# Who waits for the write of a slot of maxima: VectorE at its third fold, or ScalarE at its copy

## The reference

```
theta_x = (x[dst] - x[src]) @ theta_w.T + theta_b
phi_x   = x[src] @ phi_w.T + phi_b
e       = relu(theta_x + phi_x)
out     = segment_max(e, dst, num_segments=6250)
out     = where(isfinite(out), out, 0)
y       = layernorm(x + out)          # over the features, eps 1e-5
```

## Time and profile before

| | us |
|---|---|
| median of 3 runs (lowest, highest) | 1252.27 (1236.91, 1257.81) |
| the profiled execution's own time | 1242.66 |
| its span, from the first to the last instruction | 1240.8 |
| stage 1, up to the first fold | 111 |
| the edge loop, from the first fold (110.9) to the last (1153.0) | 1042 |
| the tail | 88 |

### The profile page before, as it was taken

One profiled execution on the slowest core, in us unless ns is written; L12 is line 12 of the kernel. 1 busy time (PEld: TensorE's weight loads), 2 busy tenths in 40 slices (PEclk: granted clock), 3 DMA queues, 4 the chain that ended last, 5 costly groups with the idle time before them and its releaser, 6 DMA issues.

```text
span 1240.8 us, 5980 instructions
## 1 busy us (share of the span) xinstructions
PE 313.0 (25%) x953; PEld 194.2 (16%) x953; DVE 518.0 (42%) x1191; ACT 274.6 (22%) x568; POOL 807.9 (65%) x840
## 2 busy tenths in 40 slices
PE   6363322444342343110000000100014342430000
PEld 5142111222121232000000000000012131210000
DVE  4002332545343454543333433543325253537698
ACT  2022132233232232321111211321101010100144
POOL 6724756766666766677765676677746667667574
PEclk9667565666566655555555555555557565656555
DMA  8567545666465665676655665776547476747264
GB/s 262 164 196 225 178 156 169 229 204 210 159 204 181 215 213 194 231 241 201 199 191 166 209 192 191 256 228 206 192 139 261 145 236 225 240 136 229 100 195 157
DMA packets 111584, 245.76 MB, mean 198 GB/s; under 512 B 19141, under 2 KB 51226, under 8 KB 111546
## 3 DMA queue, kind: packets, MB, share of 16 engines
q0 software_dynamic: 39984, 109.21, 30.8%
q1 hardware_dynamic: 71130, 135.51, 29.9%
q10 hardware_dynamic: 432, 0.66, 0.2%
HBM read 129.89 MB, written 115.45 MB: 198 GB/s over the span
## 4 chain that ended last, share of the span: by engine, by line
DVE 29%; another core or an unknown queue 27%; issue 19%; POOL 10%; PE 6%; ACT 5%; DMA 4%; DVEq 1%; SPq 0%; ACTq 0%; POOLq 0%
DVE acc L582 16%; POOL rows L315 9%; DVE hist L582 6%; ACT hist L379 3%; DMA rows<-b_table,idx 2%; DVE stats L692 1%; PE acc L411 1%; DVE a_sb L681 1%; DVE hist L689 1%; DVE reached L596 1%; DVE a_sb L676 1%; PE ps_b L427 1%; PE ps_a L411 1%; DVEq L580 1%
## 5 line engine op out<-in xcount | busy, mean ns | idle before, releaser
L315 POOL DMA_INDIRECT rows<-b_table,idx x731 | 701.3, 959 | 372.2 <-issue 208.4
L379 ACT COPY hist<-acc 128x512 f32<-128x512 f32 x253 | 147.3, 587 | 471.0 <-DVE hist L582 241.3
L582 DVE SCALAR_TENSOR_TENSOR acc<-acc,reset,rows 128x256 f32<-128x256 f32 x253 | 124.7, 493 | 116.2 <-DVE acc L582 41.9
L582 DVE SCALAR_TENSOR_TENSOR acc<-hist,reset,rows 128x256 f32<-128x256 f32 x201 | 98.7, 491 | 151.5 <-issue 52.6
L582 DVE SCALAR_TENSOR_TENSOR hist<-acc,reset,rows 128x256 f32<-128x256 f32 x253 | 122.3, 483 | 80.8 <-DVE acc L582 41.0
L427 PE MATMUL ps_b<-diff_sb,conv_t 128*128 128x256 f32 x204 | 93.7, 607 | 223.5 <-issue 119.0
L447 PE MATMUL ps_d<-hi,row_of 128*128 128x512 bf16 x98 | 48.7, 497 | 381.3 <-remote 181.1
L462 PE MATMUL ps_a<-theta_sb,xt_sb 128*128 128x256 f32 x196 | 77.6, 545 | 130.6 <-issue 77.8
L427 PEld LDWEIGHTS ps_b<-diff_sb,conv_t 128*128 128x128 f32 x204 | 54.6, 295 | 243.0 <-issue 144.6
L582 DVE SCALAR_TENSOR_TENSOR acc<-hist,reset,early 128x256 f32<-128x256 f32 x51 | 25.2, 495 | 137.5 <-ACT hist L379 93.2
L384 ACT ACTIVATE signs<-ps_d,node_up 128x782 bf16<-128x782 f32 x49 | 44.7, 912 | 151.6 <-issue 74.6
(11 more groups left out here) (120 smaller groups left out, 342.9 us busy)
## 6 DMA issues: line engine op xcount, KB each, us to landing
runmax<-hist SPq DMA_DIRECT2D x260, 384.0 KB
rows<-b_table,idx POOLq DMA_INDIRECT x731
b_table<-rows SPq DMA_DIRECT2D x7, 896.0 KB
xt_sb<-in_xt SPq DMA_DIRECT2D x49, 128.0 KB
early<-in_x SPq DMA_DIRECT2D x12, 512.0 KB
out<-hist SPq DMA_DIRECT2D x11, 512.0 KB, 2.9
xt_sb<-in_xt SPq DMA_DIRECT2D x7, 512.0 KB
xt_sb<-in_xt SPq DMA_DIRECT2D x7, 384.0 KB
```

The source lines that it names most:

```text
L315: pool.indirect_dma_start(out=rows[:, PLACE[k], :], out_offset=None, in_=b_table, in_offset=bass.IndirectOffsetOnAxis(ap=idx[:, k:k + 1], ...
L379: nc.scalar.copy(hist[:, slot:slot + n - 1, :], acc[:, at:at + n - 1, :]).then_inc(s_copied, 1)
L582: nc.vector.scalar_tensor_tensor(new, former, reset[:, k:k + 1], row_at(k), ALU.min, ALU.max).then_inc(s_fold, 1)
```

## The change

The ring of maxima gets eight groups in place of six (24 slots in place of 18, that is 6 KB more in each partition), and the ring of gathered rows keeps its 18 slots under a name of its own. VectorE's third fold no longer waits for the write of a former group, except in the last eight groups, where the first fold does. ScalarE's copy of group g waits for the write of the group that held the slots of group g + 2, which is group g + 2 - 8 = g - 6. VectorE's first fold of group g + 2 waits for that copy, so its third fold comes after the write of group g - 6 too. `AHEAD` = 2 replaces a written number at VectorE's wait for the copies, which stays as it was.

```diff
-HELD = 6
+RING = 18
+HELD = 8
+AHEAD = 2
...
-    SLOTS = HELD * GROUP
+    SLOTS = RING
...
-        hist = sb("hist", [P, SLOTS, D])
+        hist = sb("hist", [P, HELD * GROUP, D])
...
                 act.wait_ge(s_fold, STOP[g])
-                if g >= HELD:
-                    act.wait_ge(s_hout[g % HELD], 16 * (g // HELD))
+                if g + AHEAD >= HELD:
+                    act.wait_ge(s_hout[(g + AHEAD) % HELD], 16 * ((g + AHEAD) // HELD))
                 nc.scalar.copy(hist[:, slot:slot + n - 1, :], acc[:, at:at + n - 1, :]).then_inc(s_copied, 1)
...
-                if 2 <= g < LATE:
-                    dve.wait_ge(s_copied, g - 1)
+                if AHEAD <= g < LATE:
+                    dve.wait_ge(s_copied, g + 1 - AHEAD)
...
-                    if s == (n - 1 if g < LATE else 0) and g >= HELD:
+                    if s == 0 and g >= LATE:
                         dve.wait_ge(s_hout[g % HELD], 16 * (g // HELD))
```

More of the change, by code:

```diff
@@ L154, in build @@
         pos_i = hist_flat[:, 3000:3000 + STEPS].bitcast(I32)
-        assert STEPS + 2 <= 1000 and (SLOTS - 1) * D >= 3000 + STEPS
+        assert STEPS + 2 <= 1000 and (SLOTS - 1) * D >= 3000 + STEPS and SLOTS <= HELD * GROUP
         acc = ps("acc", [P, 4, D])
```

## The result

The changed kernel takes 1254.17 us, median of 20 runs (1247.11 to 1263.37). The kernel before, in the same measurement, takes 1248.35 us, median of 20 runs (1235.64 to 1257.81). The ratio is 1.0065, 95% interval 1.0036 to 1.0094: no change by the 2% bound, but 0.65% slower with an interval that excludes 1, where I had forecast 0.3% faster. The ratios here are taken over the executions within 1.5% of their kernel's fastest and not from the two medians, so the two ways can differ by some tenths of a per cent.

What follows compares the result with a forecast made beforehand. POOL's issue rate (914 us for 731 gathers) plus 119.5 us of waits for folds bound the loop. From the 1252.3 us median, 4.0 us saved and 0.1 us added gave 1248 us; eight in ten 1216 to 1266 us.

Steps and rivals of the forecast that it cites:

- the term of 4.0 us: VectorE's third folds lose a wait of 0.06 us, felt at POOL's 67 waits for folds: 4.0 us saved.
- The upper bound of 14.8 us: Most that VectorE's removed third-fold wait could save: 247 groups times 0.06 us.
- The lower bound of 0: Least that VectorE's removed third-fold wait could save: nothing reaches the end, 0 us.
- The rival in which the slow stretches spread: More groups with slowly following folds, 1.15 us of POOL each: 22 more give 1277 us, 86 more 1351 us; chance 0.09.
- The bound: The loop is POOL's issue rate, about 1.25 us a gather (914 us), plus 119.5 us waiting for VectorE's folds.
- Does the removed wait end last anywhere?: At VectorE's third folds: no, the write of maxima is not what holds them; 3.5 us slack at the tightest place.
- my 2 to 5 us: Landing time expected for a 384 KB write of maxima, from nearby DMAs.
- ScalarE's wait and the longer ring at nothing: ScalarE's copy waiting for the write of group g - 6: cost 0; longer ring's extra tail waits: below 0.1 us, hidden.
- The Trainium skill's rule: VectorE copies equally long with and without a semaphore behind each; by that the removed wait saves 0.
- the first rival: Removed wait shares in VectorE's slow folds, so they shrink: 1181 or 1177 us, a third of it 1227; chance 0.14.
- The slow stretches shrink: Third folds lose 71 us idle or POOL regains 75 us: 1181 or 1177 us, a third of it 1227; chance 0.14.
- the four signs that I named: Profile after: 0.04 us third-fold gaps, POOL's waits near 120 us, no copy released by a write, as many slow groups.

Runs made afterwards that it cites:

- 1083 condition: Series in which the kernel before took 1082 to 1084 us, in place of 1245 to 1260 us in others; the record does not say whether it was the same machine.
- 1250 condition: Series in which the kernel before took 1245 to 1260 us: the first measurement and the first, second and last of six follow-up series.
- the run above: Kernel before with 16 unused semaphore increments more per group from SyncE, 4,176 in all: 1391.12 us, ratio 1.1055 in the 1250 condition.
- the memory alone: Kernel before with six unused slots behind the ring of maxima, 6 KB, waits as before: 1246.53 us, ratio 1.0021.
- the last series: Changed kernel again beside the kernel before (1256.05 us): 1258.42 us, ratio 0.9988; a kernel with added SyncE increments was measured too.

## Why the prediction was wrong, step by step

**The step that failed is the term of 4.0 us**, 67 waits of POOL times 0.06 us, "since POOL's 67 waits are the only places where a shorter gap reaches the end". It was mis-sized: the changed kernel is 1.0065 and 0.9988 times the kernel before in one condition and 1.0005 and 1.0000 in the other, and no measurement of it shows a gain of 0.3%. The 0.06 us themselves were right (0.07 us in the 1083 condition). What was wrong is the number that they were multiplied with, and what lies behind these places.

- 36 of the 67 are gaps of 0.304 to 0.306 us, 11.0 us in all. That is the plain gap ahead of every gather, and no wait for VectorE. The 1083 condition has 53 such gaps with a fold's name, and POOL waits for nothing there. POOL's real waits, put down to folds or not, are 41 gaps with 116.6 us beyond 0.31 us each. That this sum is near my 119.5 us is luck.
- 18 of them, with 41 us, lie between 620 and 937 us, in or close behind groups whose folds start on steps of 0.70 us. I had written that the 0.06 us would not show there, and then counted them for the waits that these stretches cause.
- 20 of them, with 76 us, lie before 520 us and after 980 us. There POOL waits since VectorE has just waited for a late result of TensorE, 5.8 to 12.2 us at a time. Between 980 us and the end it is a tile of a that VectorE takes from TensorE (L631). Ahead of a wait of POOL of 5.64 us, which ends at 1064.0 us in the kernel before, VectorE stood like this:

```profile
1052.68 0.43 DVE L631 TENSOR_TENSOR a_sb<-ps_a,bias 128x256 f32<-128x256 f32 x1 [8.56 <-remote]
...
1061.78 0.42 DVE L631 TENSOR_TENSOR a_sb<-ps_a,bias 128x256 f32<-128x256 f32 x1 [7.16 <-remote]
```

The three gaps left are under 0.45 us. In the 20 places a third fold's 0.06 us may reach POOL. With one third fold each, as in my sum, that is 1.2 us; the intervals of the changed kernel in the 1250 condition are 3.6 and 4.9 us to either side, so they can't show it. In the 1083 condition POOL waits for no fold, and the term is 0.

The upper bound of 14.8 us was too high on the same ground. The lower bound of 0 left out that a shift can also cost a step. One sum was wrong as well: the runs' range of 1236.9 to 1257.8 us, shifted by 0 to 14.8 us, is 1222 to 1258 us and not 1225 to 1262.

**What the loss of 0.65% is** stays open. Its interval excludes 1, but it did not come again in the other measurement of the same two kernels in the 1250 condition (0.9988), nor in the two of the 1083 condition. The bigger tile and the eight semaphores are not needed for it, since a ring of six has 1.0051. ScalarE's wait is in every kernel made from the changed one, and five of their ratios in this condition lie below 1 (0.9969 to 0.9993).

The rival in which the slow stretches spread looks right at first: 82 slow groups against 65, and 17 x 1.15 us = 19.6 us would be nearly the 20.8 us between the two spans. The traces say otherwise. Of the 20.8 us, 6.5 lie ahead of the first gather, 3.4 in the gathers' own time (704.7 against 701.3 us), 4.1 in all of POOL's idle time between the first gather and the last, and 6.0 between the last gather and the last fold, where VectorE is still behind from a wait of 9.31 us for a tile of TensorE's (L633), which ended at 1149.03 us. The tail has the rest. So more slow groups did not become POOL's waits. In eleven traces the first gather starts at 100.5 to 112.6 us; this part alone, which the change does not touch, differs by more than the medians' 5.8 us.

**The bound.** "POOL's issue rate plus 119.5 us of waits for folds" was right as the sum of that trace, and wrong as a property of the program. In the 1083 condition the same kernel has none of the 119.5 us. The stretches of the earlier trace rows and the long wait of the earlier trace rows are one thing, increments that come late. In the earlier trace rows, TensorE's matmul of L427 ended at 387.46 us and its increment came at 395.44 us. Its transpose (L437) ended at 387.89 us and the increment came at 398.95 us, ScalarE's copy started at 398.98 us, and TensorE ran again at 399.40 us. In the loop of this trace 120 increments of TensorE are recorded: 51 come within 0.06 us, 30 come 5 to 10 us late and 20 more than 10 us, the longest 22.3 us. Of VectorE's 434, 250 come within 0.06 us, 76 come 0.5 to 0.9 us late and 41 come 1.3 to 2.0 us late. All 130 of ScalarE come within 0.01 us. With SyncE's increments it is as with VectorE's, by the run above. What makes them late is not known.

**Does the removed wait end last anywhere?** No, as predicted. No copy of ScalarE is put down to a write of maxima in the changed kernel:

```profile
L381 ACT COPY hist<-acc x253: 574/586/621, 119.6 to 1139.8; 128x512 f32<-128x512 f32 x127
...
  DVE hist L584: 229.5, 80
  issue: 110.7, 59
  DVE acc L584: 107.9, 27
  remote: 32.1, 13
```

These names are a weak sign by themselves. The traces of the 1250 condition hold only a part of the semaphores' records, and 72 of these waits have no named releaser. The times settle it. The write lands in 2.8 us in the 1083 condition, inside my 2 to 5 us. For the 1250 condition the page gives no landing time, but the trace of the kernel before holds 631 of the 4,176 increments of these writes: their median is 2.5 us behind the issue, and the last is 5.3 us behind it. In the changed kernel it is 712, with a median of 2.5 us and a longest of 5.9 us. No third fold before comes less than 8.56 us behind the issue of the write that it waits for, and no copy after comes less than 8.9 us behind it.

**ScalarE's wait and the longer ring at nothing:** nothing speaks against it, within 0.3%. The ring of six (1.0051) and of eight (1.0065) with the same removed wait, and the memory alone (1.0021, 0.9986 to 1.0057), don't come apart by their intervals.

**The Trainium skill's rule**, "VectorE: DVE Perf Modes", section "The DRAIN you can't avoid", by which the sum would have been 0 saved, gave the better number for the end, by luck. It speaks of the signal behind an instruction. The second wait ahead of one does cost 0.06 to 0.07 us here; the sum of 0 came out since nothing of that reached the end. The Trainium skill's rule beside the first rival ("Perfetto Trace Analysis", section "DMA Instruction — HWDGE (DVE, Sync)"), that a DMA's semaphore may come late when it writes to HBM, is not borne out for these writes: 2.8 us, and at most 6.4 us in any trace that I read for it. Where third folds did wait for a write, behind 16 increments in SyncE's queue, it was issued late and not landed late.

**The slow stretches shrink** fell: 82 slow groups, and 63 in the last series, against 65. **Three of the four signs that I named** came as for the forecast: 0.04 us, POOL's waits within 25 us, no copy released by a write. The fourth, about as many groups with long gaps, came in the last series (63 against 65) and less so in the first measurement (82). They could not tell a gain of 4 us from a loss of 6, and a list of signs for a forecast of 0.3% should say so.

## What to carry to other kernels

Price a removed instruction by what stands behind it where the waits fall, not by its own gap where the engine catches up: 0.06 us in front of an event that came on steps of 0.70 us was worth nothing here, or a step either way. Before counting waits, look how long each of them is: 36 of 67 "waits" were the 0.31 us that stood ahead of every gather. Before counting them as headroom, look whether the engines of one chain start at even distances with nothing to wait for, and measure the kernel again later: here 165 us of 1250 were not the program's. And an interval from runs of one measurement does not hold what differs between measurements: the same edit gave 1.0065 and 0.9988 in one condition, each with an interval of 0.3 to 0.4%.

## What the runs showed of the hardware that was not expected

- The same kernel took 1245.26 us and, later, 1082.07 us on chips of the same number. A lower TensorE clock is not the reason: the granted clock was 0.549 in the 1083 condition (changed kernel), and 0.571 and 0.574 in the 1250 condition. In the latter, increments of semaphores come late. Its traces also have far fewer records of semaphores (4,132 updates against 21,385, both of the changed kernel), so whether the recording takes part can't be told. The difference stands in every execution of a series, not only in those whose trace is kept. Why a machine is in one condition or the other stayed open.
- Two increments that SyncE issues start 0.06 us apart in one condition (3,915 distances in 239.9 us) and 0.26 us apart at the mean in the other (1000.5 us), most of that in steps of 0.70 us and more. 4,176 increments that nobody waits for cost nothing that could be measured in the 1083 condition (1.0003, 0.9994 to 1.0013) and 10.6% in the 1250 condition. In the latter run VectorE's own increments came in time. Whether fewer increments would make the kernel faster in the 1250 condition was not measured: the kernels with joined and split writes never met it.
- A second wait of a VectorE instruction costs 0.07 us where nothing else holds it (26.2 against 8.9 us over 247 folds, and the same 26.2 us in the kernel with split writes).
- With 12 gathers ahead or 24, POOL's waits for VectorE are the same 119 to 126 us, in the 1250 condition.
